# A decoder layer on one core: input product of a state scan moved from GpSimd to VectorE, first expert tiles without gates, and a new order of work

## Time and profile before

| what | value |
|---|---|
| median of 3 runs | 583.9 us (582.71 to 586.61) |
| the profiled execution | 587.0 us, span 585.2 us |
| busy: PE / PEld / DVE / ACT / POOL | 430.1 / 312.3 / 405.9 / 223.9 / 204.3 us |
| share of the span | 73 / 53 / 69 / 38 / 35 % |
| DMA | 70.10 MB, mean 120 GB/s |

### The profile page before, as it was taken

The page is one execution under the profiler, slowest core; times in us unless marked ns, Lnnn a source line. Parts: engine busy times, 40 slices in busy tenths (PEclk is TensorE's granted clock), DMA queues, the critical chain, the costliest instruction groups (busy, mean ns, idle before and its releaser), DMA issues.

```text
span 585.2 us, 18602 instructions
## 1 busy us (share of the span) xinstructions
PE 430.1 (73%) x8286; PEld 312.3 (53%) x8286; DVE 405.9 (69%) x536; ACT 223.9 (38%) x418; POOL 204.3 (35%) x117
## 2 busy tenths in 40 slices
PE   4486068886946578857665579625899999999993
PEld 2334056553635544534444555212578888888883
DVE  1643978999984689998994047999987686333336
ACT  2486075556363235357323226502152522222220
POOL 2331157869050013542114001421634354444440
PEclk9876557675975679876765559777999999999997
DMA  8767445574130014333212003752134444555402
GB/s 260 249 217 228 161 166 166 149 197 167 55 94 4 4 50 95 77 76 74 39 24 57 4 5 85 229 206 64 72 121 168 144 174 158 172 181 178 146 1 72
DMA packets 29580, 70.10 MB, mean 120 GB/s; under 512 B 4946, under 2 KB 7708, under 8 KB 29500
## 3 DMA queue, kind: packets, MB, share of 16 engines
q1 hardware_dynamic: 29339, 68.87, 37.9%
q0 software_dynamic: 160, 0.04, 0.1%
HBM read 54.54 MB, written 14.35 MB: 118 GB/s over the span
## 4 chain that ended last, share of the span: by engine, by line
PE 43%; DVE 35%; issue 14%; DMA 2%; ACT 2%; SPq 2%; POOL 1%; DVEq 1%; ACTq 0%
DVE arena_h L1345 12%; PE bank L755 10%; DVE arena_h L1354 7%; PE bank L966 4%; PE bank L943 4%; PE bank L962 4%; PE bank L963 4%; PE bank L944 4%; PE bank L945 4%; PE bank L745 3%; DMA w_hl<-in_w 2%; PE bank L948 2%; DVE tmp_o L1396 2%; SPq L566 2%; PE bank L727 1%
## 5 line engine op out<-in xcount | busy, mean ns | idle before, releaser
L687 POOL TENSOR_TENSOR arena_s<-du,bc 128x1024 f32<-128x1024 f32 x32 | 88.3, 2762 | 216.8 <-DMA bc<-scr_x 181.4
L692 POOL TENSOR_TENSOR hg_lo<-vkp,hg_hi 128x512 fp32r<-128x512 f32 x50 | 70.7, 1414 | 88.6 <-DVE hg_hi L1578 88.6
L1345 DVE TENSOR_TENSOR_SCAN arena_h<-arena_s 128x1024 f32<-128x1024 f32 x32 | 87.9, 2746 | 6.6 <-DVE arena_h L1354 4.5
L745 PE MATMUL bank<-arena_h,const 128*128 128x512 f32 x128 | 84.1, 794 | 8.6 <-DVEq L1356 8.2
L1212 ACT ACTIVATE vkp<-bank,b 128x512 f32<-128x512 f32 x50 | 34.4, 689 | 117.4 <-PE bank L945 108.3
L755 PE MATMUL bank<-vkp,tiles 32*32 32x32 f32 (+1 forms) x3072 | 44.7, 213 | 46.9 <-issue 30.2
L755 PEld LDWEIGHTS bank<-vkp,tiles 32*32 32x32 f32 x3072 | 40.8, 133 | 52.8 <-issue 33.7
L1574 DVE TENSOR_TENSOR vkp<-vkp,bank 128x512 f32<-128x512 f32 x50 | 34.3, 686 | 48.5 <-ACT vkp L1212 46.7
L1070 ACT ACTIVATE arena_s<-delta,negA 128x510 f32<-128x510 f32 x64 | 43.0, 713 | 58.5 <-DVEq L1346 57.9
L1354 DVE TENSOR_TENSOR arena_h<-arena_h,bc 128x1024 f32<-128x1024 f32 x32 | 56.6, 1768 | 12.2 <-PE bank L745 8.3
L678 POOL TENSOR_TENSOR w_hl<-w_hl 128x512 fp32r<-128x512 f32 x25 | 42.3, 1709 | 60.4 <-ACT w_hl L1205 60.4
(11 more groups left out here) (160 smaller groups left out, 742.1 us busy)
## 6 DMA issues: line engine op xcount, KB each, us to landing
w_ring<-scr_w SPq DMA_DIRECT2D x50, 512.0 KB, 3.3
bc<-scr_x SPq DMA_DIRECT2D x32, 512.0 KB, 5.0
scr_w<-w_hl SPq DMA_DIRECT2D x25, 512.0 KB, 3.0
w_hl<-in_w SPq DMA_DIRECT2D x25, 256.0 KB, 3.8
xT<-in_x_t SPq DMA_DIRECT2D x1, 1024.0 KB, 7.6
xres<-in_x_tok SPq DMA_DIRECT2D x1, 1024.0 KB, 9.7
out<-xres SPq DMA_DIRECT2D x8, 128.0 KB, 1.8
wqkvb<-in_wqkvb SPq DMA_DIRECT2D x1, 784.0 KB, 5.5
```

The source lines that it names most:

```text
L687: pool.tensor_tensor(dBu[:, i % 2, :].rearrange("p (e t) -> p e t", e=2), du[:, :, GT_ * th:GT_ * th + GT_], bc[:, i % NBC, 0, :].unsqueez ...
L692: pool.tensor_tensor(hg_lo[i % 2][:, :], hrel[:, i % 2, :], hg_hi[i % 2][:, :], ALU.subtract).then_inc(s_hglo, 1)
L745: mm = pe.matmul(o[:, :], ident, hC[i % NHC][:, GT_ * et:GT_ * et + GT_], start=(n == 0), stop=(n == DS - 1))
L1345: link(dve.tensor_tensor_scan(hst, dA[:, i % 2, :], dBu[:, i % 2, :], 0.0, ALU.mult, ALU.add))
```

## The change

Parts, in the order of the diff:
- Plan: many durations are new (P .8 to 1.5, base .6 to 1.05, O 1.1 to 1.6, UW 1.6 to 1.9, solve 6.4 and 5.0 to 7.5 and 6.4, dt_rows 3.6 to 6.7). Batches begin elsewhere: `BEGIN`. Ties are decided by the way plus a bonus per stage, `AHEAD`.
- v of all batches and beta of all tokens (16 rows, 4 products) are computed at the start; beta goes to DRAM and back, spread over 128 rows (16 DMAs per batch, beside the 8 for `binst`). It multiplies the triangular matrix in place of the mask, no longer k.
- Clamps of the squared sums go: their minimum becomes a bias and a bound in the same instruction as the normalising product.
- Softplus' last four instructions of each half go from VectorE to GpSimd; ACT gets one more.
- `du * B` goes from GpSimd to VectorE. Input, scan and product with C are all in place, in `hst`, a ring of four (`NHC`). B and C rows have five buffers instead of three.
- Weight staging has two buffers (`NWS`) instead of three, and the plan puts a load after the input product of the same number.
- The first two tiles of each half (`FREE` = 352 // 128) have no gates: no gate product on TensorE, none on VectorE, and no wait for the gates.

```diff
-NWS = 3
-NHC = 3
+NWS = 2
+FREE = NSH * DFF // P
+NHC = 4
-HOP = 0.12
-NBC = 3
+HOP = 0.15
+NBC = 5
+BEGIN = {1: ("act", "kn"), 2: ("pe", "UW1"), 3: ("dve", "solve2"), "dt": ("dve", "P3"), "scan": ("dve", "qn")}
+AHEAD = {("attention", 0): -10, ("attention", 1): -10, ("attention", 3): 230, ("experts", 0): 40, ("experts", 1): -160, ("middle", 0): 240, ("middle", 1): 50, ("ssm", 0): 10}
...
-            k = min(open_, key=lambda k: (ways[k][0], -way[k]))
+            k = min(open_, key=lambda k: (ways[k][0], -way[k] - AHEAD.get(stage(*k[1:]), 0)))
...
-    if b % 2:
-        on = [*on, ("act", "tile_u", b - 1)]
+    if b in BEGIN:
+        on = [*on, (*BEGIN[b], b - 1)]
...
-        r = op("sp", "wraw", g, .3, [staged[g - NWS][1]] if g >= NWS else [], lag=3.5)
+        r = op("sp", "wraw", g, .3, [staged[g - NWS][1] if g >= NWS else None, ("dve", "dbu", g)], lag=3.5)
...
-        dbu[i] = op("pool", "dbu", i, 2.5, [bc, dve_, scan.get(i - 2)])
-        scan[i] = op("dve", "scan", i, 2.4, [decay, dbu[i], add.get(i - 1)])
-        add[i] = op("dve", "add", i, 1.25, [scan[i], bc, sums.get(i - 3)])
+        dbu[i] = op("dve", "dbu", i, 1.1, [bc, dve_, sums.get(i - NHC)])
+        scan[i] = op("dve", "scan", i, 2.35, [decay, dbu[i], (*BEGIN["scan"], 0) if i == 0 else None])
+        add[i] = op("dve", "add", i, 1.1, [scan[i], bc])
...
+            def spread_beta(b):
...
+                for h in range(HH):
+                    sp.dma_start(beta_kc[x][DH * h:DH * h + DH, :], scr_b[b, h, :].partition_broadcast(DH)).then_inc(s_beta[x], 16)
...
+            def softplus(et):
+
+                pool.wait_ge(s_sp, et + 1)
+                link(pool.tensor_tensor(sp_w, sp_w, sp_z, ALU.subtract))
+                link(pool.tensor_tensor(sp_l, sp_l, sp_w, ALU.subtract))
+                link(pool.tensor_tensor(delta[:, et, :], delta[:, et, :], sp_l, ALU.add))
...
+                pool.tensor_tensor(du[:, et, :], delta[:, et, :], u[:, et, :], ALU.mult).then_inc(s_du, 1)
...
+                if ft == FREE:
                     pe.wait_ge(s_gstk, th + 1)
...
+            def inputs(i):
...
+                link(dve.tensor_tensor(hst[i % NHC].rearrange("p (e t) -> p e t", e=2), du[:, :, GT_ * th:GT_ * th + GT_],
+                                       bc[:, i % NBC, 0, :].unsqueeze(1).broadcast_to([P, 2, GT_]), ALU.mult))
+
             def scan(i):
                 dve.wait_ge(s_dA, 2 * (i + 1))
-                dve.wait_ge(s_dbu, i + 1)
-                link(dve.tensor_tensor_scan(hst, dA[:, i % 2, :], dBu[:, i % 2, :], 0.0, ALU.mult, ALU.add))
+                h = hst[i % NHC]
+                link(dve.tensor_tensor_scan(h, dA[:, i % 2, :], h, 0.0, ALU.mult, ALU.add))
...
-                if name in ("ssk", "ssq"):
-                    signal(dve.tensor_scalar(r, take(k)[:, :], 1e-24, None, ALU.max),
-                           s_clamp[x], 2 * n + (name == "ssq") + 1, k)
...
             def hidden_gated(i):
-                k = ("G", i)
-                o = take(k)
...
+                if i % FT >= FREE:
+                    k = ("G", i)
+                    link(dve.tensor_tensor(h, h, take(k)[:, :], ALU.mult))
+                    free(k)
```

More of the change, by code:

```diff
@@ L68, with stage @@
 PAD = C * C + C
-NWS = 3
-NHC = 3
+NWS = 2
+FREE = NSH * DFF // P
+NHC = 4
 RING = 8
-HOP = 0.12
-NBC = 3
+HOP = 0.15
+NBC = 5
 BLOCK, FETCH = 256, 3.75
+BEGIN = {1: ("act", "kn"), 2: ("pe", "UW1"), 3: ("dve", "solve2"), "dt": ("dve", "P3"), "scan": ("dve", "qn")}
+AHEAD = {("attention", 0): -10, ("attention", 1): -10, ("attention", 3): 230, ("experts", 0): 40, ("experts", 1): -160, ("middle", 0): 240, ("middle", 1): 50, ("ssm", 0): 10}
+SSM = ("decay0", "decay1", "dbu", "scan", "add", "padd", "sum", "bc")
+MIDDLE = ("gate", "yT", "ynorm", "x3T", "split", *(f"gates{part}" for part in range(GATE_PARTS)))
+EXPERTS = ("hid", "relu", "mul", "lo", "out", "wload")
+OTHER = ("xe", "conv", "silu", "wb", "b", "beta_st", "dt_rows", "dtlo", "rows", "zero", "dt", "wraw", "whi", "wlo", "wst", "y_out", "sel",
+         "b2", "fin", "nst", "nap", "outs")
+def stage(name, i):
+    if name in SSM:
+        return "ssm", i // DS
+    if name in MIDDLE:
+        return "middle", i
+    if name in EXPERTS:
+        return "experts", i // FT
+    return ("else", 0) if name in OTHER else ("attention", i)
 class Plan:
@@ L328, in decoder_layer @@
     turns, order = PLAN.turns, PLAN.order
+    v_order = [which for name, which in order["act"] if name == "v"]
     scr_w = nc.dram_tensor("scr_w", (FT, P, 2, 2 * D), F32).ap()
@@ L503, in decoder_layer @@
         s_scan = sem("s_scan")
-        s_dbu = sem("s_dbu")
         s_hc = sem("s_hc")
@@ L635, in fetch_sel @@
             def fetch_sel():
+                for s in range(NWS):
+                    sp.wait_ge(s_kept[s], 16 * ((FT - 1 - s) // NWS + 1))
                 for x in range(2):
@@ L646, in _ @@
             for name, which in order["sp"]:
-                if name == "move_b":
-                    move_b(which)
+                if name == "beta_st":
+                    keep_beta()
+                elif name == "beta":
+                    spread_beta(which)
                 elif name == "rows":
@@ L729, in dt_rows, with betas @@
                     filled(k, mm)
+            def betas():
+                pe.wait_ge(s_ld_c, LD_C)
+                for th in range(NG):
+                    k = ("b", th)
+                    o = fill(k)
+                    for kt in range(KT):
+                        mm = pe.matmul(o[0:H, :], wqkvb[:, kt, 3 * D:3 * D + H], xT[:, kt, GT_ * th:GT_ * th + GT_],
+                                       start=(kt == 0), stop=(kt == KT - 1))
+                    filled(k, mm)
             def dt_all(et):
@@ L1033, in conv_rows, with betas @@
                 act.nop().then_inc(s_xpad, 1)
+            def betas():
+                for th in range(NG):
+                    k = ("b", th)
+                    signal(act.activation(at_g[th][0:H, :], take(k)[0:H, :], ACT.Sigmoid), s_sig, th + 1, k)
+                nc.scalar.preload_act_table_set(LN_EXP)
             def silu(et):
@@ L1596, in _ @@
                     row_copies()
-                elif name == "dt":
-                    softplus(which)
                 elif name == "zero":
                     begin()
+                elif name == "dbu":
+                    inputs(which)
                 elif name == "scan":
```

291 lines of the change are left out of this document (148 added, 143 removed).

## The result

The kernel after takes 557.4 us in the median of four runs (553.9 to 563.8), the kernel before beside it 585.3; ratio 0.9496, 95% interval 0.9436 to 0.9557. Timed again later it gave 0.9529 (0.9475 to 0.9584). The forecast was 545, faster: the sign is right, the gain was put 12 us too high. The profiled execution took 563.8 us, the longest of the four, for a span of 562.0; a second profiled one has a span of 558.8.

What follows compares the result with a forecast made beforehand. Order, two queues waiting in turn, was taken to bound the kernel before 403 us, TensorE from 492 on. VectorE's path gave 538, TensorE's 356+6+14+145+6+14 = 541 to 555; forecast 545, range 520 to 590.

Steps and rivals of the forecast that it cites:

- What bounds that part is an order: Before 403 us neither TensorE nor VectorE is full; two queues take turns waiting, VectorE idle 110.1 us up to 492.
- TensorE's path: First expert product at 356 us instead of 403.49, end at 541, or 555 if leftover sums do not fit the gap.
- 28+227+66+35: TensorE up to the first expert product: start 28, busy 227, gaps 66 after small products, other waits 35 (from 62): 356 us.
- VectorE's path: Up to the second half's gates: 28 + 360.6 busy + 62 idle = 451 us instead of 492; end 538.
- The input product: 32 products du by B on VectorE: 39.4 us at 1.23 each, plus 6.4 hand-overs; collisions with GpSimd fall from 31.9 to 18.
- Two ungated tiles: Each half's first two expert tiles run ahead of the gates on TensorE, 2 x 3.02 = 6.0 us.
- The signs: Trace readings named beforehand as showing the forecast right or wrong, such as first expert product at 345 to 365 us.
- Five cover it: Five B and C row buffers (27 us at 5.4 a scan) cover 24 small DMAs per batch, 10 us, on SP.
- B: Rival: experts start late through weight staging, or gates stay on the path; up to 25 us more, 570; chance 0.12.
- C: Rival: VectorE's idle time falls to 30 us, its path gives 506, TensorE holds the end at 515 to 524; chance 0.08.
- D: Rival: the change only swaps engines, VectorE's idle time stays at 110 us, 586, no change; chance 0.07.
- E: Rival: slower, GpSimd collisions cost VectorE 71 us instead of 18; 591 to 606, middle 598; chance 0.13.

Runs made afterwards that it cites:

- an order alone: Kernel before with only the planner changed: bonuses searched for it, staging tied to GpSimd's input product, new durations and hand-overs; 574.5 us, ratio 0.9820.
- durations alone: Kernel before, its planner given the kernel after's durations for attention blocks and dt_rows, hand-over 0.15 for 0.12, only the order changing; 594.1 us, ratio 1.0164.
- the run with copies: Kernel before with 16 unread DRAM-to-DRAM copies of 256 KB put into SP's queue behind the load of rows 24; 591.1 us, ratio 1.0106.
- The run with GpSimd: Kernel after with the scan's input product back on GpSimd, in place, all other work in the same order; 569.5 us, ratio 0.9754.

## Why the prediction was right, and where it was off

- **What bounds it: right.** "What bounds that part is an order". Without its bonuses the new kernel keeps 1.0 of the 4.9%; an order alone brings 1.8% in the old one. That the two don't add up to 4.9 shows that the worth of an order depends on the work it is made for. The forecast kept no sum for order apart from idle time, and durations alone would have been its weakest part: they cost 1.6%.
- **TensorE's path decides: right, and the miss is in one term.** Forecast: first expert product at 356, end at 541. Measured: 381.8 and 562.0. Behind the first expert product 185 us were forecast (541 - 356), 180.2 came. The 25.8 us ahead of it are: busy 233.2 against 227 (+6.2), gaps 72.2 + 2.3 + 1.4 = 75.9 against 66 (+9.9), other waits 44.7 against 35 (+9.7). The sum that read "28+227+66+35" is what missed: other waits fell from 62.7 to 44.7, two thirds of what I gave them, and the gaps rose where I left them as they were. The long gaps of the kernel after, five above 3 us, all stand where the DMA share is 0.33 to 0.55, and the new order puts the weight staging and the rows beside attention (DMA share 0.35 to 0.40 in 180 to 313, 0.24 before). That this is their cause is likely after the run with copies, but no run took the staging away from there and kept the rest.
- **The busy term was off by only 6.2 us by luck.** I took three states' sums off TensorE ahead of the first expert product (8 us) and 12 us of v and beta. Measured: three more states' sums stand there (31 instead of 28; 85.8 us, 76.5 before), and all other products there fell by 23.0 us, 14.5 of them the products for k, q, v and beta. So one part came out 17 us too low and the other 11 us too high.
- **VectorE's path: two errors of opposite sign, and it doesn't decide.** Forecast up to the second half's gates: 360.6 busy, 62 idle, 451. Measured to 459.4: 274.05 + 18.16 + 40.89 = 333.1 busy and 98.3 idle. Idle time in 28 to 95 fell from 25 to 22 instead of 12, in 313 to 403 from 37 to 23 instead of 15. Some of the difference is one of counting: hand-overs, 6.4 us in my busy time, stand in the rows as idle. The gates at 459.4 are 16 us ahead of TensorE's need. I had also read the gates at 492 as what lets the last stretch begin. In the kernel before they were done 1.9 us ahead of their first product, and TensorE, busy for 86.24 of the 89 us up to 492, waited there only 2.1 us, for GpSimd's low parts and a sum. So both paths met there, and a shorter path of VectorE alone could have gained next to nothing.
- **The input product: size right (1.33 mean, 1.23 undisturbed), collisions better than forecast** (10.7 us, I took 18). The forecast gave the move no gain of its own. The run with GpSimd prices it at 2.2 to 2.6%, within an order that was made for VectorE.
- **Two ungated tiles, 6.0 us:** 6.7 with their gate products. Right. Softplus' move: no difference that can be told, where I had counted 13.7 us less on VectorE.
- **The signs.** GpSimd's busy time (136.9 for about 135) and the scans at 2.29 us came out. The first expert product (381.8 for 345 to 365) and VectorE's busy time (387.5 for 395 to 425) did not. "No single VectorE wait of 15 us for a transposed block" came true to the letter only: a wait of 15.19 us now stands in front of an input product. The ring of four waits there for a sum that stands behind small products on TensorE and their pauses; I had costed the looser ring at nothing. "Scans running beside expert tiles" is wrong for this kernel, whose bonuses put all scans ahead of the tiles. And a sign of being wrong nearly came: VectorE is idle 98.3 us before the second half's gates, near the 110 named. The time fell even so, as VectorE's path doesn't decide.
- **"Five cover it" for the rows: true, and three do too**, once the order is made for three.
- **Rivals.** Of B, the late staging did not occur: the wait for weights ahead of the first expert product is 0.18 us. Its other half did in part: the first half's gates hold TensorE for 6.5 and 1.4 us between the two ungated tiles and the gated ones. C asked for 30 us of idle time on VectorE and D for 110; measured were 98.3, and D's time did not come with them. E fell by the collisions: the trace of the kernel after has scans of 3.25 us at most. The rule of the Trainium skill that it stood on (page "SBUF — State Buffer", section "SBUF: two separate sides": an exclusive lock for the whole instruction) holds for the pairs that meet, and the input product that left GpSimd was most of those. With it back there, the cost was back at 30.6 us.

What stays open: what sets the pauses of TensorE, and with them how the orders end within 2% of each other. The two profiled executions with the least time in pauses are also the two shortest (62.6 at a span of 546.9, 57.9 with softplus' tail on VectorE at 550.3), but each is one execution, and why one order or one execution has fewer was not tried. Nor were the clamps, the beta products and the earlier v undone by themselves, so the 14.4 us of busy time that the changed work took off TensorE are not told apart by experiment.

## What to carry to other kernels

When a list scheduler writes the order, judge an edit only after the order has been made anew for it: two buffers seemed to be worth 4.4% and were worth nothing. A product whose collisions hold up a busy neighbour may be worth moving onto that neighbour: VectorE's three steps grew by 19.6 us, and the kernel was faster, in an order made for it. Read where the last wait before the full stretch ends, not the busy share; and look whether the engine behind a path really waited for it. And add up the idle and busy time of the engine that decides over the whole span, as sums moved from behind a point to ahead of it change nothing by themselves.

## What the runs showed of the hardware

TensorE pauses after each 128 small products (weight load and matmul each). Without DMA traffic in it the pause is 1.0 to 2.5 us long; among 16 copies of 256 KB, two pauses of 1.62 and 1.92 us became 5.18 and 5.21. In the kernel after it is up to 6.53, at a DMA share of 0.51. Traffic can lengthen it but need not: one of 1.73 us had a share of 0.89. The page of the profile lists a DMA queue of kind "instruction" (65 packets, 1.06 MB in the kernel after), which fits blocks of instructions queued behind data, though that they wait in the same engines was not shown by itself. The Trainium skill, page "Runtime: NRT & Kernel Launch", section "Instruction fetch mechanics", has blocks of 256 instructions fetched by a DMA queue of the engine's own and calls the fetch hidden; the block agrees (128 products are 128 weight loads and 128 matmuls), the hiding does not, for products as small as these. The second surprise is GpSimd's input product in the run that moved it back: the same 128x1024 product takes 2.34 us at the least and 3.12 on average beside VectorE, and VectorE's scans beside it 2.79 instead of 2.44, so a collision is paid on both engines.
